# Last phase of a three-layer fp32 kernel: token tiles turned by VectorE blocks and SBUF transfers in place of TensorE transposes

## The chip, the cores and the metric

One core of one Trainium2 chip runs the whole kernel. The metric is the device time in microseconds (us); lower is better.

## What is computed

4096 tokens of width 256 pass through an attention layer, a differential cross attention and a mixture of experts, each followed by a residual sum and a layer norm. Only the last part matters here. It routes every token to two of four experts (a gated one "sw" with 1024 hidden columns, an "me" and a "ce" expert with 512, and an "ml" expert with 1024):

```python
e0 = jax.nn.silu(x @ sw_w1) * (x @ sw_w3) @ sw_w2
e1 = jax.nn.gelu(sym @ me_c1w + me_c1b, approximate=False) @ me_c2w + me_c2b
h2 = _layer_norm(syn + attn, ce_n1g, ce_n1b)
ff = jax.nn.relu(h2 @ ce_f1w + ce_f1b) @ ce_f2w + ce_f2b
h2 = _layer_norm(h2 + ff, ce_n2g, ce_n2b)
e2 = h2 @ ce_gen_w + ce_gen_b
e3 = jax.nn.gelu(x @ ml_w1 + ml_b1, approximate=False) @ ml_w2 + ml_b2
return (rw[..., None] * gathered).sum(axis=2)
```

## The kernel before, in words

Three phases run one after the other with overlaps: phase_a and phase_b are the two attention layers, phase_c is the experts. The change lies in phase_c alone. It works on `NP` = 8 "pairs" of 512 tokens. X1 holds all tokens with tokens on partitions; the matmuls need them with features on partitions, so tiles must be turned.

Every engine runs a program of its own, whose order is written out by hand. For a pair j each engine goes through `work(j, i)` for 24 chunks i of 128 hidden columns: chunks 0 to 7 are sw, 8 to 11 ce, 12 to 15 me, 16 to 23 ml. In chunk i TensorE makes `first(j, i)` (six matmuls of 512 columns, twelve for sw), ScalarE applies the activation into GF, VectorE multiplies in the gate for sw and splits the result into a high and a low fp32r half, GH (a cast at L2257 and a subtraction at L2259). TensorE then runs the second layer of chunk i-3 (`LAG` = 3), `second(24j+i-3)`: twelve matmuls of 256 columns that add up in the banks 4 and 5. Every product is made of three matmuls (`mm3`: high by high, high by low, low by high), all of which share the line L109. A first() waits for the activation that frees its bank, a second() for its GH, and the first second() of an expert also for VectorE to have taken the sums of the expert before out of the banks: `second(24j+12)` waits for `ff_add(j)` (VectorE, chunk 14), and `second(24j+16)` waits for `add_expert(j, 1)` (VectorE, chunk 18).

Three tiles a pair are turned by TensorE, each with eight 128x128 transposes into two PSUM banks; ScalarE then copies them out as the high half and VectorE subtracts to get the low half:

- `load_x(j+1)` in chunk 23 of pair j (L1881, ScalarE L2039, VectorE L2106) turns the next pair's tokens into XC, of which there is one buffer. After it TensorE runs second(24j+21) and then `synergy(j+1)`, 24 matmuls that wait for the low half.
- `turn_n(j)` in chunk 5 (L1905, L2075, L2202) turns the normalised tile NN into NTh and NTl, for chunk 8.
- `gen_turn(j)` in chunk 20 (L1914, L2080, L2202) turns the normalised residual RR, for `generate(j)` in chunk 22, 24 matmuls.

VectorE has more to do at fixed chunks: in chunk 0 the statistics of NN, in 1 its normalisation (`center`, L2158), in 2 to 4 the routing and the output norm of the pair before, in 10 and 18 an expert's sums times the routing weight (L2211), in 11 to 13 the bias rows (`add_bias`, L2219; in pair 0 in chunks 19 and 21, and instead the splits of late weights), in 14 `ff_add` (L2243), in 15 the statistics of RR and in 16 its normalisation after a wait for GpSimd's root. SyncE in this phase only stores each finished pair (after `center` in chunk 4 of the next). Pair 0 runs its first eleven chunks among the last steps of phase_b.

Of the kernel before, what the change touches and what calls it, by code (L numbers as in the profile page):

```python
# [1716 lines left out]

def in_bank(j):
    return (3, 2) if j == 0 else (7, 6)


def phase_c(M, b_end):
# [28 lines left out]
    RS = put("RSc", [128, 4])  # L1751
    XH = Place(M, 65536)("XC", [128, 2, 2, TOK], F32R)
    NN = Place(M, 81920)("NN", [128, 4, 256])
# [8 lines left out]
    d_g = {step: M.sem(f"c_g{step}") for step in LOADS}  # L1762
    d_out = M.sem("c_out")
    pe_x = M.sem("c_pe_x")
    pe_syn = M.sem("c_pe_syn")
    pe_nt = M.sem("c_pe_nt")
    pe_gt = M.sem("c_pe_gt")
    pe_gen = M.sem("c_pe_gen")
# [24 lines left out]
    dve_add = M.sem("c_dve_add")  # L1793
    dve_ff = M.sem("c_dve_ff")
    dve_seq = M.dve_seq
    pool_w = M.sem("c_pool_w")
# [9 lines left out]
    def split(w, name, q):  # L1806
# [18 lines left out]
    def sync(e):  # L1825
        w = Passed(e)

        def ask(name, q, sem):
            if name in ("sw_w1", "sw_w3", "ml_w1"):
                i = a[name].rearrange("(k p) n -> p k n", k=2)[:, :, 512 * q:512 * q + 512]  # L1830
            elif name in ("ce_f1w", "ce_gen_w"):
                i = a[name].rearrange("(k p) n -> p k n", k=2)
            else:
                i = a[name].rearrange("(k p) n -> p k n", p=128)[:, 4 * q:4 * q + 4, :]
            dma(e, RAW[name, q][:, :, :], i, sem)

        def early(s):
            if s == 238:
                for end in gathered:
                    w.wait_ge(*end)  # L1840
                for o, i in ((BC[:, 1:3, :], a["BC"][:, 1:3, :]), (bf, a["BC"][:, 3, :]), (RB[:, :, :], a["RB"]), (gc[:, :, :], a["gc"])):
                    dma(e, o, i, d_tc)
                w.wait_ge(b_end["values"], 112)
                w.wait_ge(*b_end["projected"])
            if s == 243:
                w.wait_ge(b_end["scores"], 240)
            if s == 258:
                w.wait_ge(b_end["scores"], 256)
                w.wait_ge(b_end["values"], 128)
            if s == 259:  # L1850
                w.wait_ge(b_end["folds"], 14)
            if s == 278:
                w.wait_ge(*b_end["output"])
                w.wait_ge(dve_br, 1)
            for way in LOADS.get(s, ()):
                ask(*way, d_g[s])

        def rest():
            for j in range(NP - 1):
                w.wait_ge(dve_ctr, out_stats(j) + 1)  # L1860
                dma(e, out_tm[:, 4 * j:4 * j + 4, :], X1[:, 4 * j:4 * j + 4, :], d_out)
            for u in range(2):
                t = 4 * NP - 4 + 2 * u
                w.wait_ge(dve_ctr, 3 * NP + u)
                dma(e, out_tm[:, t:t + 2, :], X1[:, t:t + 2, :], d_out)
            w.wait_ge(d_out, 16 * (NP + 1))

        return early, rest

    def tensor(e):  # L1870
# [3 lines left out]

        def load_x(j):
            w.wait_ge(b_end["normalised"], j + 1)
            for c, b in enumerate(in_bank(j)):
                if j:
                    w.wait_ge(*free[b])
                for i in range(4):  # L1880
                    t = e.transpose(P[b][:, 128 * i:128 * i + 128], X1[:, 4 * j + i, 128 * c:128 * c + 128], ident)  # L1881
                t.then_inc(pe_x, 1)
                free[b] = (dve_x, 2 * j + c + 1)

        def synergy(j):
            w.wait_ge(dve_x, 2 * j + 2)
            split(w, "ce", 0)
            wt = W["ce", 0]
            for i, b in enumerate(syn_banks(j)):
                if b > 3:  # L1890
                    w.wait_ge(*free[b])
                else:
                    w.wait_ge(act_g, 24 * (j - 1) + b + 21)
                for k in range(2):
                    t = mm3(e, P[b][:, 0:260], XH[:, k, 0, 128 * i:128 * i + 128], XH[:, k, 1, 128 * i:128 * i + 128],
                            wt[:, 0, k, :], wt[:, 1, k, :], k == 0, k == 1)
                t.then_inc(pe_syn, 1)
                free[b] = (dve_syn, 4 * j + i + 1)

        def turn_n(j):  # L1900
            w.wait_ge(dve_ctr, syn_stats(j) + 1)
            for c in range(2):
# [3 lines left out]
                t.then_inc(pe_nt, 1)  # L1906
                free[7 - c] = (dve_nt, 2 * j + c + 1)

        def gen_turn(j):
            w.wait_ge(dve_ctr, ff_stats(j) + 1)  # L1910
            for c in range(2):
                w.wait_ge(*free[7 - c])
                for i in range(4):
                    t = e.transpose(P[7 - c][:, 128 * i:128 * i + 128], RR[:, i, 128 * c:128 * c + 128], ident)  # L1914
                t.then_inc(pe_gt, 1)
                free[7 - c] = (dve_gt, 2 * j + c + 1)

# [24 lines left out]
        def first(j, i):  # L1942
            x, hc = chunk(i)
            b = first_bank(i)
            hi, lo = XH[:, :, 0, :], XH[:, :, 1, :]
            if x == "sw":
# [47 lines left out]
        def work(j, i):  # L1994
            first(j, i)
            if i == 5:
                turn_n(j)
            if i == 20:
                gen_turn(j)
            if i == 22:  # L2000
                generate(j)
            if i >= LAG:
                if i < 23 or j + 1 < NP:
                    second(24 * j + i - LAG)
            elif i and j:
                second(24 * j + i - LAG)
            if i == 23 and j + 1 < NP:
                load_x(j + 1)
                second(24 * j + 21)

        def early(s):
            if s == INPUT:
                load_x(0)
            if s == SYNERGY:
# [16 lines left out]
    def scalar(e):  # L2031
        w = Passed(e)

        def load_x(j):
            w.wait_ge(b_end["scores"], 240)
            w.wait_ge(pe_a, 24 * j)
            for c, b in enumerate(in_bank(j)):
                w.wait_ge(pe_x, 2 * j + c + 1)
                e.activation(XH[:, c, 0, :], P[b], ACT.Copy).then_inc(act_x, 1)  # L2039

# [12 lines left out]
        def work(j, i):  # L2053
# [16 lines left out]
            if i == 5:  # L2070
                w.wait_ge(b_end["folds"], 14)
                w.wait_ge(pe_gen, 4 * j)
                for c in range(2):
                    w.wait_ge(pe_nt, 2 * j + c + 1)
                    e.activation(NTh[:, c, :], P[7 - c], ACT.Copy).then_inc(act_nt, 1)  # L2075
            if i == 20:
                w.wait_ge(pe_a, 24 * j + 12)
                for c in range(2):
                    w.wait_ge(pe_gt, 2 * j + c + 1)
                    e.activation(NTh[:, c, :], P[7 - c], ACT.Copy).then_inc(act_gt, 1)  # L2080
            if i == 23 and j + 1 < NP:
                load_x(j + 1)
            if j == 0 and i in CHUNK_TAKES:
                take(*CHUNK_TAKES[i])

        def early(s):
            if s == INPUT + 1:
                load_x(0)
            if s in EARLY:
# [9 lines left out]
    def vector(e):  # L2099
        w = Passed(e)  # L2100
        seq = Chain(w, dve_seq)

        def load_x(j):
            for c, b in enumerate(in_bank(j)):
# [29 lines left out]
        def synergy(j):  # L2134
            w.wait_ge(dve_rb, 1)
            w.wait_ge(b_end["folds"], 9)
            w.wait_ge(b_end["values"], 128)
            w.wait_ge(pe_nt, 2 * j)
            for i, b in enumerate(syn_banks(j)):
# [58 lines left out]

        def turned(landed, j, done):
            for c in range(2):  # L2200
                w.wait_ge(landed, 2 * j + c + 1)
                e.tensor_tensor(NTl[:, c, :], P[7 - c], f32(NTh[:, c, :]), ALU.subtract).then_inc(done, 1)  # L2202

# [25 lines left out]
        def scaled(j):  # L2229
            w.wait_ge(dve_ctr, syn_stats(j) + 1)  # L2230
            w.wait_ge(pe_gt, 2 * j)
            w.wait_ge(*b_end["turned"])
# [13 lines left out]
        def work(j, i):  # L2246
# [18 lines left out]
            if i == 1:  # L2265
                center(syn_stats(j), NN)
            if i == 2:
                route(j)
# [4 lines left out]
            if i == 5:  # L2273
                turned(act_nt, j, dve_nt)
            if i == 20:
                turned(act_gt, j, dve_gt)
# [29 lines left out]
        def early(s):  # L2306
            if s == INPUT + 1:
                load_x(0)
            if s in DVE_TAKES:
# [258 lines left out]
```

## Time and profile before

| what | value |
|---|---|
| time, median of 3 runs | 1552.7 us (1552.16 to 1553.82) |
| span of the profiled execution | 1550.1 us |
| TensorE busy / share | 1502.6 us / 97% |
| VectorE busy / share | 1139.4 us / 74% |
| ScalarE busy / share | 847.5 us / 55% |
| mean granted TensorE clock | 0.993 |

The profiled execution is listed with its span, from the first to the last instruction; its own time is not listed apart. The median of the runs is 2.6 us above the span, which is what lies around the span. Times in the views count from the span's start. Steady pairs of phase_c repeat every 88 us from about 925 us on; the pair between 1013 us and 1101 us is looked at closely.

### The profile page before, as it was taken

How to read it: one execution, taken by the hardware profiler on the slowest of the kernel's cores; microseconds unless marked ns; L12 is line 12 of the kernel's file. 1: busy time of each engine (PE TensorE's matmuls, PEld its weight loads, DVE VectorE, ACT ScalarE, POOL GpSimd, SP SyncE). 2: the span in 40 equal slices, each digit the busy share in tenths (PEclk: the TensorE clock that was granted, in tenths of full speed). 3: DMA queues.
4: the chain of work that ended last, by engine and by line, in shares of the span. 5: the costliest groups of instructions: out<-in, count | busy, mean ns of one | idle time of the engine just before them, and what ended most of it. 6: DMA issues, size and time to landing. Idle time of an engine off the chain costs nothing.

```text
span 1550.1 us, 28824 instructions
## 1 busy us (share of the span) xinstructions
PE 1502.6 (97%) x11288; PEld 1065.1 (69%) x11288; DVE 1139.4 (74%) x2305; ACT 847.5 (55%) x1123; POOL 372.8 (24%) x404
## 2 busy tenths in 40 slices
PE   8999999899999999999999999999999999999998
PEld 4333333335566666666656898888989898888887
DVE  6445555548799999999967877777676767777675
ACT  5888889876688888888863421222222221222221
POOL 1000000124556667666453300000000000000000
PEclk9999999999899999999999999999999999999999
DMA  7656665446565666657652100000000000000000
GB/s 153 137 112 117 122 121 103 71 95 113 95 93 88 105 89 98 110 78 96 93 169 69 62 1 15 1 14 1 1 15 1 14 1 15 1 15 1 1 14 14
DMA packets 61576, 97.37 MB, mean 63 GB/s; under 512 B 12461, under 2 KB 29881, under 8 KB 61441
## 3 DMA queue, kind: packets, MB, share of 16 engines
q1 hardware_dynamic: 61312, 95.34, 33.3%
q8 instruction: 89, 1.46, 0.4%
q14 instruction: 47, 0.38, 0.1%
q10 hardware_dynamic: 128, 0.20, 0.0%
HBM read 26.29 MB, written 4.19 MB: 20 GB/s over the span
## 4 chain that ended last, share of the span: by engine, by line
PE 84%; DVE 8%; ACT 3%; SPq 3%; issue 2%; DMA 1%; POOLq 0%; DVEq 0%; POOL 0%; ACTq 0%
PE ps L109 79%; SPq L119 3%; PE ps L1277 2%; DVE NM L1495 2%; ACT H L614 1%; ACT PX L1438 1%; DVE EE L758 1%; PE ps L1239 1%; DVE XC L2106 1%; PE ps L1285 1%; PE ps L1914 0%; DMA ST<-QS 0%; PE ps L1905 0%; PE ps L1209 0%; DVE QS L678 0%
## 5 line engine op out<-in xcount | busy, mean ns | idle before, releaser
L1495 DVE TENSOR_REDUCE NM<-ps 128x4 f32<-128x1024 f32 x256 | 307.5, 1219 | 29.2 <-PE ps L109 27.7
L1438 ACT ACTIVATE PX<-ps 128x1024 f32<-128x1024 f32 x256 | 262.2, 1024 | 80.2 <-PE ps L109 79.0
L614 ACT ACTIVATE H<-ps,b1c 128x1024 f32<-128x1024 f32 x256 | 268.2, 1118 | 48.6 <-PE ps L109 47.0
L2066 ACT ACTIVATE GF<-ps,cols 128x512 f32<-128x512 f32 x128 | 88.2, 689 | 295.7 <-PE ps L109 295.6
L109 PE MATMUL ps<-XC,W_sw_w 128*128 128x512 f32 x768 | 185.8, 393 | 0.0
L2257 DVE CAST GH<-GF 128x512 fp32r<-128x512 f32 x192 | 82.0, 427 | 106.9 <-ACT GF L2066 101.8
L109 PEld LDWEIGHTS ps<-XC,W_sw_w 128*128 128x128 f32 x768 | 140.5, 188 | 28.0
L2365 POOL TENSOR_SCALAR RSc<-AGc 128x4 f32<-128x4 f32 x23 | 6.9, 298 | 599.5 <-DVE AGc L2152 599.5
L109 PE MATMUL ps<-PX,VT 128*32 128x256 f32 x2048 | 138.6, 388 | 0.1
L2259 DVE TENSOR_TENSOR GH<-GF,GH 128x512 fp32r<-128x512 f32 x192 | 133.2, 694 | 6.6
L109 PE MATMUL ps<-KT,QT 48*128 48x512 f32 x512 | 128.1, 498 | 3.7 <-DVE NM L1495 1.8
L2061 ACT ACTIVATE GF<-ps 128x512 f32<-128x512 f32 x64 | 38.0, 596 | 169.2 <-PE ps L109 169.2
L109 PE MATMUL ps<-H,w2p 128*32 128x512 f32 x1024 | 124.8, 605 | 3.0 <-ACT XF L1407 1.1
L109 PE MATMUL ps<-QT,KT 52*128 52x256 f32 x1024 | 109.2, 290 | 4.7 <-ACT PX L1438 3.8
L109 PEld LDWEIGHTS ps<-QT,KT 52*128 52x128 f32 x1024 | 90.1, 187 | 26.1 <-ACT PX L1438 10.7
L109 PE MATMUL ps<-W_ml_w,GH 128*128 128x256 f32 x768 | 103.6, 285 | 0.2
L758 DVE TENSOR_SCALAR EE<-ps,b2p 128x512 f32<-128x512 f32 x63 | 47.1, 747 | 77.0 <-PE ps L109 76.9
L109 PEld LDWEIGHTS ps<-KT,QT 48*128 48x128 f32 x512 | 47.8, 184 | 80.7 <-issue 60.2
L109 PEld LDWEIGHTS ps<-W_sw_w,GH 128*128 128x128 f32 x768 | 100.0, 191 | 4.5
L109 PE MATMUL ps<-W_sw_w,GH 128*128 128x256 f32 x768 | 102.7, 283 | 0.0
L109 PEld LDWEIGHTS ps<-W_ml_w,GH 128*128 128x128 f32 x768 | 98.0, 191 | 5.8 <-issue 3.4
L109 PE MATMUL ps<-ST,w1s 48*128 48x512 f32 x512 | 96.5, 451 | 5.3 <-ACT H L614 2.0
(240 smaller groups left out, 2560.3 us busy)
## 6 DMA issues: line engine op xcount, KB each, us to landing
KT<-KS SPq DMA_DIRECT2D x128, 192.0 KB, 4.7
ST<-QS SPq DMA_DIRECT2D x254, 96.0 KB, 2.8
QT<-XSb SPq DMA_DIRECT2D x128, 96.0 KB, 4.2
XT<-in_xT_dram SPq DMA_DIRECT2D x8, 512.0 KB, 4.1
raw_a<-in_x_dram SPq DMA_DIRECT2D x8, 512.0 KB, 4.3
CR<-in_ctxT_dram SPq DMA_DIRECT2D x8, 512.0 KB, 4.7
out_dram<-X SPq DMA_DIRECT2D x7, 512.0 KB, 2.9
R_sw_w<-in_sw_w_dram SPq DMA_DIRECT2D x6, 512.0 KB, 5.5
```

What stands on the lines that cost most here:

```text
L109: return e.matmul(o, l, r, start=start, stop=stop, skip_group_check=True)
L119: e.dma_start(o, i).then_inc(sem, 16)
L614: e.activation(H1[s % 8][:, :, :], PP[s % 3][:, :, :], ACT.Tanh, bias=b1c[:, half:half + 1], scale=1.0).then_inc(act_th, 1)
L758: e.tensor_scalar(EE[:, j % 4, :], P[6][:, :], b2p[:, 0:1], None, ALU.add).then_inc(dve_ee, 1)
L1239: t = e.transpose(low[0:32, 128 * qc:128 * qc + 128], f32(NS2[u % 2][:, 4 * qc:4 * qc + 4, :, :]).rearrange("p g l n -> p (g l n)"), ident)
L1277: t = e.transpose(P[7][:, 256 * qc + 128 * i:256 * qc + 128 * i + 128], OT[f][:, i, 128 * qc:128 * qc + 128], ident)
L1438: e.activation(PX[s % 3][:, :, :, :], PP[2][:, :, :].rearrange("p g (c q) -> p g c q", c=2), ACT.Exp, bias=0.0, scale=0.25).then_inc(act_e ...
L1495: e.tensor_reduce(NM[u % 2][:, qc, :, :, i], PP[qc][:, :, :].rearrange("p g (m k) -> p g m k", m=2), AX.X, ALU.max, negate=True).then_inc( ...
L2061: e.activation(g[:, :], o, ACT.Silu, bias=0.0, scale=1.0).then_inc(act_g, 1)
L2066: e.activation(g[:, :], o, f, bias=cols[:, col:col + 1], scale=1.0).then_inc(act_g, 1)
L2257: e.tensor_copy(h[:, 0, :], g[:, :]).then_inc(dve_h, 1)
L2259: e.tensor_tensor(h[:, 1, :], g[:, :], f32(h[:, 0, :]), ALU.subtract).then_inc(dve_h, 1)
```

## The change

Of the three turns a pair, 22 of 24 no longer use TensorE (pair 0 keeps its own load_x and turn_n). Each is now: one VectorE transpose of the 128x1024 tile in blocks of 32x32 into the new tile TT; sixteen transfers from SBUF to SBUF that put the blocks in place in the new tile XR (32 partitions, two rows of 512 bytes each, 32 KB a transfer); ScalarE's copy and VectorE's subtraction as before, but out of XR in SBUF and in runs of 32 elements.

- The turn of NN: VectorE's block in chunk 1 behind `center`, sixteen transfers by SyncE, copies in chunk 5 as before.
- The turn of the next pair's tokens: VectorE's block in chunk 8, sixteen transfers by SyncE, copies (`next_x`) in chunk 13, on VectorE ahead of add_bias. XC has two buffers. `load_x` leaves chunk 23, and second(24j+21) moves behind the next pair's synergy and its first(0).
- The turn of RR: VectorE's block in chunk 16 behind `center`, twelve transfers by SyncE and four by ScalarE (behind its activation of chunk 17, after a wait for the block), copies in chunk 20 as before.

The scratch size given to the program shrinks from its default to 1024, which makes room for TT, XR and the second XC.

```diff
+TURN_X, SPLIT_X = 8, 13
+SHARED = 3
...
+    put = Place(M, 176192)
+    XH = [Place(M, 65536)("XC0", [128, 2, 2, TOK], F32R), put("XC1", [128, 2, 2, TOK], F32R)]
+    TT = put("TT", [128, 8, 4, 32])
+    XR = put("XR", [128, 2, TOK])
...
+    def as_turned(ap):
+        return ap.rearrange("p (v a t) -> p a v t", v=4, a=4)
+    def turned(c):
+        return XR[:, c, :].rearrange("p (a v t) -> p a v t", a=4, v=4)
+    def blocks(e, rows):
+        for a in rows:
+            for b in range(4):
+                dma(e, XR[32 * b:32 * b + 32, :, 128 * a:128 * a + 128],
+                    TT[32 * a:32 * a + 32, b::4, :, :].rearrange("p c v t -> p c (v t)"), d_turn)
...
         def rest():
-            for j in range(NP - 1):
-                w.wait_ge(dve_ctr, out_stats(j) + 1)
-                dma(e, out_tm[:, 4 * j:4 * j + 4, :], X1[:, 4 * j:4 * j + 4, :], d_out)
+            for j in range(NP):
+                if j:
+                    w.wait_ge(dve_turn, n_turn(j))
+                    w.wait_ge(dve_gt, 2 * j)
+                    blocks(e, range(4))
+                    w.wait_ge(dve_ctr, out_stats(j - 1) + 1)
+                    dma(e, out_tm[:, 4 * j - 4:4 * j, :], X1[:, 4 * j - 4:4 * j, :], d_out)
+                if j + 1 < NP:
+                    w.wait_ge(dve_turn, x_turn(j + 1))
+                    w.wait_ge(dve_nt, 2 * j + 2)
+                    blocks(e, range(4))
+                w.wait_ge(dve_turn, r_turn(j))
+                w.wait_ge(dve_nt, 2 * j + 2)
+                w.wait_ge(dve_x, 2 * min(j + 2, NP))
+                blocks(e, range(SHARED))
...
             first(j, i)
-            if i == 5:
-                turn_n(j)
-            if i == 20:
-                gen_turn(j)
+            if i == 5 and not j:
+                turn_n()
                     second(24 * j + i - LAG)
-            elif i and j:
+            elif j:
                 second(24 * j + i - LAG)
-            if i == 23 and j + 1 < NP:
-                load_x(j + 1)
-                second(24 * j + 21)
...
+        def next_x(j):
+            w.wait_ge(b_end["normalised"], NP)
+            w.wait_ge(pe_a, 24 * (j - 1))
+            w.wait_ge(d_turn, 256 * x_turn(j))
+            for c in range(2):
+                e.activation(as_turned(XH[j % 2][:, c, 0, :]), turned(c), ACT.Copy).then_inc(act_x, 1)
...
                 w.wait_ge(pe_a, 24 * j + 12)
+                w.wait_ge(d_turn, 256 * r_turn(j))
                 for c in range(2):
-                    w.wait_ge(pe_gt, 2 * j + c + 1)
-                    e.activation(NTh[:, c, :], P[7 - c], ACT.Copy).then_inc(act_gt, 1)
-            if i == 23 and j + 1 < NP:
-                load_x(j + 1)
+                    e.activation(as_turned(NTh[:, c, :]), turned(c), ACT.Copy).then_inc(act_gt, 1)
+            if i == SPLIT_X and j + 1 < NP:
+                next_x(j + 1)
+            if i == 17:
+                w.wait_ge(dve_turn, r_turn(j))
+                w.wait_ge(dve_nt, 2 * j + 2)
+                w.wait_ge(dve_x, 2 * min(j + 2, NP))
+                blocks(e, range(SHARED, 4))
...
+        def next_x(j):
+            hi, lo = XH[j % 2][:, :, 0, :], XH[j % 2][:, :, 1, :]
+            for c in range(2):
                 w.wait_ge(act_x, 2 * j + c + 1)
-                e.tensor_tensor(XH[:, c, 1, :], P[b], f32(XH[:, c, 0, :]), ALU.subtract).then_inc(dve_x, 1)
+                e.tensor_tensor(as_turned(lo[:, c, :]), turned(c), f32(as_turned(hi[:, c, :])), ALU.subtract).then_inc(dve_x, 1)
+        def turn(n, tile):
+            w.wait_ge(d_turn, 256 * (n - 1))
+            e.transpose(TT[:, :, :, :].rearrange("p b v t -> p v b t"), tile.rearrange("p v (b t) -> p v b t", b=8)).then_inc(dve_turn, 1)
...
                 center(syn_stats(j), NN)
+                if j:
+                    turn_n(j)
...
-            if i == 23 and j + 1 < NP:
-                load_x(j + 1)
+            if i == TURN_X and j + 1 < NP:
+                turn_x(j + 1)
+            if i == SPLIT_X and j + 1 < NP:
+                next_x(j + 1)
...
                 center(ff_stats(j), RR)
+                turn_r(j)
...
-    nc = bacc.Bacc("TRN2", target_bir_lowering=False, num_devices=1)
+    nc = bacc.Bacc("TRN2", target_bir_lowering=False, num_devices=1, dynamic_dma_scratch_size=1024)
```

## Rows read from the trace of the kernel before

**Rows 1.** The page: busy time and share of the span of each engine, instructions.
```profile
PE 1502.6 (97%) x11288; PEld 1065.1 (69%) x11288; DVE 1139.4 (74%) x2305; ACT 847.5 (55%) x1123; POOL 372.8 (24%) x404
```
**Rows 2.** One stretch of phase_c: length, busy per engine, granted clock, DMA share, GB/s.
```profile
1000.00:1100.00 100.00, 99.80 (x641) 89.88 (x640) 68.86 (x168) 24.29 (x38) 4.42 (x6) 1.00 0.02 6
```
**Rows 3.** Chain of waits through one pair: start, length, what.
```profile
1010.89 0.45 PE ps L1881 x4
...
1038.72 0.87 PE ps L1905 x8
...
1085.27 0.87 PE ps L1914 x8
...
1098.92 0.45 PE ps L1881 x4
```
**Rows 4.** Instruction groups by line, phase_c: busy us, mean ns, idle before.
```profile
L1914 PE MATMUL ps<-C,RR 128*128 128x128 f32 x64 | 8.3, 272 | 0.0
...
L1881 PE MATMUL ps<-C,X 128*128 128x128 f32 x56 | 7.2, 272 | 0.0
L1905 PE MATMUL ps<-C,NN 128*128 128x128 f32 x56 | 7.2, 272 | 0.0
```
**Rows 5.** Timeline at a pair's end: start, length, engine, instructions, idle before.
```profile
1101.37 2.93 PEld L109 LDWEIGHTS ps<-W_ce,XC 128*128 128x128 f32 x24 [0.35 <-DVE XC L2106]
```
**Rows 6.** Instruction groups by line, VectorE, phase_c.
```profile
L2233 DVE TENSOR_TENSOR RR<-NN,BC 128x1024 f32<-128x1024 f32 x7 | 8.5, 1218 | 0.0
```
**Rows 7.** Timeline of VectorE, start of chunk 2, and chunks 8 and 9.
```profile
1026.24 0.69 DVE L2253 TENSOR_TENSOR GF<-GF,ps 128x512 f32<-128x512 f32 x1 [0.24 <-PE ps L109]
...
1052.05 0.69 DVE L2259 TENSOR_TENSOR GH<-GF,GH 128x512 fp32r<-128x512 f32 x1
1054.41 0.43 DVE L2257 CAST GH<-GF 128x512 fp32r<-128x512 f32 x1 [1.67 <-ACT GF L2066]
```
**Rows 8.** Timeline, chunks 13 to 15 (ScalarE, VectorE, TensorE), and chunk 14 of pair 0.
```profile
1065.22 0.69 ACT L2066 ACTIVATE GF<-ps,cols 128x512 f32<-128x512 f32 x1 [2.13 <-PE ps L109]
...
1066.40 0.69 DVE L2259 TENSOR_TENSOR GH<-GF,GH 128x512 fp32r<-128x512 f32 x1
1067.01 1.67 DVE L2219 SCALAR_TENSOR_TENSOR X<-BR,PB,X 128x256 f32<-128x256 f32 x4
...
1069.83 1.28 DVE L2243 TENSOR_TENSOR RR<-ps,RR 128x512 f32<-128x512 f32 x2
1071.58 0.43 DVE L2257 CAST GH<-GF 128x512 fp32r<-128x512 f32 x1 [0.47 <-ACT GF L2066]
...
1070.66 1.67 PE L109 MATMUL ps<-W_me_c2w,GH 128*128 128x256 f32 x12
...
892.70 0.43 DVE L2257 CAST GH<-GF 128x512 fp32r<-128x512 f32 x1 [0.47 <-ACT GF L2066]
```
**Rows 9.** Timeline, chunks 16 to 22 (VectorE, ScalarE, TensorE).
```profile
1076.56 1.38 DVE L2158 TENSOR_SCALAR RR<-RR,AGc,RSc 128x256 f32<-128x256 f32 x4 [0.93 <-POOL RSc L2367]
...
1079.40 0.69 ACT L2066 ACTIVATE GF<-ps,cols 128x512 f32<-128x512 f32 x1 [2.13 <-PE ps L109]
...
1081.19 1.65 DVE L2211 SCALAR_TENSOR_TENSOR X<-ps,PB,X 128x256 f32<-128x256 f32 x4
...
1082.21 1.67 PE L109 MATMUL ps<-W_ml_w,GH 128*128 128x256 f32 x12
...
1091.62 0.40 PE L109 MATMUL ps<-W_ce_gen_w,NTh 128*128 128x256 f32 x2
```
**Rows 10.** DMA issues by tile (ns min/median/max); landing of the 32 KB transfers WS (us).
```profile
L119 SPq DMA_DIRECT2D ST<-QS x254: 567/593/1848, 11.6 to 298.3; - x127
L119 ACTq DMA_DIRECT2D ST<-QS x2: 687/810/932, 13.0 to 13.8; - x2
...
L119 SPq DMA_DIRECT2D out_dram<-X x9: 372/372/392, 951.0 to 1547.5; - x9
...
DMA to landing us min/median/max: 1.9/2.7/3.7
```

More of the change, by code:

```diff
@@ L1715, in syn_banks @@
     return (2, 3, 6, 7) if j == 0 else (7, 6, 2, 3)
-def in_bank(j):
-    return (3, 2) if j == 0 else (7, 6)
+IN_BANKS = (3, 2)
+TURN_X, SPLIT_X = 8, 13
+SHARED = 3
 def phase_c(M, b_end):
@@ L1763, in phase_c @@
     d_out = M.sem("c_out")
+    d_turn = M.sem("c_turn")
     pe_x = M.sem("c_pe_x")
@@ L1766, in phase_c @@
     pe_nt = M.sem("c_pe_nt")
-    pe_gt = M.sem("c_pe_gt")
     pe_gen = M.sem("c_pe_gen")
@@ L1794, in phase_c @@
     dve_ff = M.sem("c_dve_ff")
+    dve_turn = M.sem("c_dve_turn")
     dve_seq = M.dve_seq
@@ L1813, in split, with n_turn, x_turn, r_turn @@
             w.wait_ge(pool_w, [*POOL_TAKES.values()].index((name, q)) + 1)
+    def as_turned(ap):
[7 more added lines that the diff above has]
+                    TT[32 * a:32 * a + 32, b::4, :, :].rearrange("p c v t -> p c (v t)"), d_turn)
+    def n_turn(j):
+        return max(3 * j, 0)
+    def x_turn(j):
+        return 3 * j - 2
+    def r_turn(j):
+        return 3 * j + 2 if j + 1 < NP else 3 * j + 1
     def syn_stats(j):
@@ L1873, in tensor, with load_x @@
         free[0] = free[1] = (b_end["folds"], 12)
[L1875 to L1879, printed above, removed]
+        def load_x():
+            w.wait_ge(b_end["normalised"], 1)
+            for c, b in enumerate(IN_BANKS):
                 for i in range(4):
-                    t = e.transpose(P[b][:, 128 * i:128 * i + 128], X1[:, 4 * j + i, 128 * c:128 * c + 128], ident)
+                    t = e.transpose(P[b][:, 128 * i:128 * i + 128], X1[:, i, 128 * c:128 * c + 128], ident)
                 t.then_inc(pe_x, 1)
-                free[b] = (dve_x, 2 * j + c + 1)
+                free[b] = (dve_x, c + 1)
         def synergy(j):
@@ L1906, in turn_n @@
                 t.then_inc(pe_nt, 1)
[L1907 to L1916, printed above, removed]
+                free[7 - c] = (dve_nt, c + 1)
         def generate(j):
@@ L2004, in work @@
                     second(24 * j + i - LAG)
-            elif i and j:
+            elif j:
                 second(24 * j + i - LAG)
-            if i == 23 and j + 1 < NP:
-                load_x(j + 1)
-                second(24 * j + 21)
         def early(s):
             if s == INPUT:
-                load_x(0)
+                load_x()
             if s == SYNERGY:
@@ L2032, in scalar, with load_x @@
         w = Passed(e)
-        def load_x(j):
+        def load_x():
             w.wait_ge(b_end["scores"], 240)
[L2036 to L2039, printed above, removed]
+            for c, b in enumerate(IN_BANKS):
+                w.wait_ge(pe_x, c + 1)
+                e.activation(XH[0][:, c, 0, :], P[b], ACT.Copy).then_inc(act_x, 1)
+        def next_x(j):
[4 more added lines that the diff above has]
+                e.activation(as_turned(XH[j % 2][:, c, 0, :]), turned(c), ACT.Copy).then_inc(act_x, 1)
         def take(name, q):
@@ L2072, in work @@
                 w.wait_ge(pe_gen, 4 * j)
+                if j:
+                    w.wait_ge(d_turn, 256 * n_turn(j))
                 for c in range(2):
-                    w.wait_ge(pe_nt, 2 * j + c + 1)
-                    e.activation(NTh[:, c, :], P[7 - c], ACT.Copy).then_inc(act_nt, 1)
+                    if j:
+                        e.activation(as_turned(NTh[:, c, :]), turned(c), ACT.Copy).then_inc(act_nt, 1)
+                    else:
+                        w.wait_ge(pe_nt, c + 1)
+                        e.activation(NTh[:, c, :], P[7 - c], ACT.Copy).then_inc(act_nt, 1)
             if i == 20:
                 w.wait_ge(pe_a, 24 * j + 12)
+                w.wait_ge(d_turn, 256 * r_turn(j))
                 for c in range(2):
-                    w.wait_ge(pe_gt, 2 * j + c + 1)
-                    e.activation(NTh[:, c, :], P[7 - c], ACT.Copy).then_inc(act_gt, 1)
-            if i == 23 and j + 1 < NP:
-                load_x(j + 1)
+                    e.activation(as_turned(NTh[:, c, :]), turned(c), ACT.Copy).then_inc(act_gt, 1)
[6 more added lines that the diff above has]
+                blocks(e, range(SHARED, 4))
             if j == 0 and i in CHUNK_TAKES:
@@ L2087, in early @@
             if s == INPUT + 1:
-                load_x(0)
+                load_x()
             if s in EARLY:
@@ L2101, in vector, with load_x, turn_n, turn_x @@
         seq = Chain(w, dve_seq)
-        def load_x(j):
-            for c, b in enumerate(in_bank(j)):
-                w.wait_ge(act_x, 2 * j + c + 1)
-                e.tensor_tensor(XH[:, c, 1, :], P[b], f32(XH[:, c, 0, :]), ALU.subtract).then_inc(dve_x, 1)
+        def load_x():
+            for c, b in enumerate(IN_BANKS):
+                w.wait_ge(act_x, c + 1)
+                e.tensor_tensor(XH[0][:, c, 1, :], P[b], f32(XH[0][:, c, 0, :]), ALU.subtract).then_inc(dve_x, 1)
+        def next_x(j):
+            hi, lo = XH[j % 2][:, :, 0, :], XH[j % 2][:, :, 1, :]
+            for c in range(2):
+                w.wait_ge(act_x, 2 * j + c + 1)
+                e.tensor_tensor(as_turned(lo[:, c, :]), turned(c), f32(as_turned(hi[:, c, :])), ALU.subtract).then_inc(dve_x, 1)
+        def turn(n, tile):
+            w.wait_ge(d_turn, 256 * (n - 1))
+            e.transpose(TT[:, :, :, :].rearrange("p b v t -> p v b t"), tile.rearrange("p v (b t) -> p v b t", b=8)).then_inc(dve_turn, 1)
+        def turn_n(j):
+            w.wait_ge(dve_ctr, syn_stats(j) + 1)
+            turn(n_turn(j), NN[:, :, :])
+        def turn_x(j):
+            w.wait_ge(b_end["normalised"], j + 1)
+            turn(x_turn(j), X1[:, 4 * j:4 * j + 4, :])
+        def turn_r(j):
+            w.wait_ge(dve_ctr, ff_stats(j) + 1)
+            turn(r_turn(j), RR[:, :, :])
         def take(name, q):
@@ L2137, in synergy @@
             w.wait_ge(b_end["values"], 128)
-            w.wait_ge(pe_nt, 2 * j)
+            w.wait_ge(pe_nt, 2 if j else 0)
+            w.wait_ge(dve_turn, n_turn(j - 1))
             for i, b in enumerate(syn_banks(j)):
@@ L2197, in route3, with low_n, low_r @@
             e.tensor_tensor(PB[:, :, :], LS[:, :, :], SL[:, :, :], ALU.mult).then_inc(dve_pb, 1)
-        def turned(landed, j, done):
+        def low_n(j):
             for c in range(2):
-                w.wait_ge(landed, 2 * j + c + 1)
-                e.tensor_tensor(NTl[:, c, :], P[7 - c], f32(NTh[:, c, :]), ALU.subtract).then_inc(done, 1)
+                w.wait_ge(act_nt, 2 * j + c + 1)
+                if j:
+                    e.tensor_tensor(as_turned(NTl[:, c, :]), turned(c), f32(as_turned(NTh[:, c, :])), ALU.subtract).then_inc(dve_nt, 1)
+                else:
+                    e.tensor_tensor(NTl[:, c, :], P[7 - c], f32(NTh[:, c, :]), ALU.subtract).then_inc(dve_nt, 1)
+        def low_r(j):
+            for c in range(2):
+                w.wait_ge(act_gt, 2 * j + c + 1)
+                e.tensor_tensor(as_turned(NTl[:, c, :]), turned(c), f32(as_turned(NTh[:, c, :])), ALU.subtract).then_inc(dve_gt, 1)
         def add_expert(j, k, n, count):
@@ L2230, in scaled @@
             w.wait_ge(dve_ctr, syn_stats(j) + 1)
-            w.wait_ge(pe_gt, 2 * j)
+            w.wait_ge(dve_turn, r_turn(j - 1) if j else 0)
             w.wait_ge(*b_end["turned"])
@@ L2266, in work @@
                 center(syn_stats(j), NN)
+                if j:
+                    turn_n(j)
             if i == 2:
@@ L2307, in early @@
             if s == INPUT + 1:
-                load_x(0)
+                load_x()
             if s in DVE_TAKES:
```

14 lines of the change are left out of this document (6 added, 8 removed).

## The prediction

> **What bounds the kernel now.** I read the page first: TensorE is busy for 97% of the span [rows 1]. The windows then show where the change lies: in a stretch of the last phase TensorE is busy for 99.80 of 100 us at a granted clock of 1.00 (the 2.4 GHz level), VectorE for 68.86, ScalarE for 24.29, and the DMA engines for 2% [rows 2]. So an instruction that leaves TensorE's queue there gives its time back, unless a wait takes its place. The chain of waits through one pair shows the two inner turns as eight transposes and 0.87 us each [rows 3]; the groups give their counts, 64, 56 and 56, which is eight transposes in each of 8, 7 and 7 turns [rows 4].
>
> **What is removed.** The change takes out 8 turns of RR, 7 of NN and 7 of the next tokens: 22 x 0.87 = 19.1 us. At a pair's end TensorE also stood still before synergy: the weight load waited 0.35 us for the low half of XC [rows 5]. That half is now made ten chunks earlier; 7 x 0.35 = 2.5 us. Gross gain 21.6 us. The twelve matmuls of second(24j+21) are only moved, and synergy waits for none of its banks: load_x needed the sums of generate out of the same two at the same place, and the activation of chunk 23 is over by then.
>
> **What is added on VectorE.** The trace has no VectorE transpose. Its nearest row by size is the 128x1024 tensor_tensor at 1.218 us [rows 6]; I take T = 1.22 us, with 0.85 (twice the 0.43 us of a 128x512 cast [rows 7]) and 2.4 (two passes) as ends. The copies and subtractions out of XR are taken at what they cost now, runs of 32 or not: ScalarE 0.6 us, VectorE 0.69 us alone and 0.64 us in a row, as in ff_add, two in 1.28 [rows 8]. An estimate by the Trainium skill, which has the block transposing one element per cycle and lane (Vector Engine (DVE) Microarchitecture Reference, "The reshape front-end and per-opcode configuration"), lands near T as well; no run here shows it yet.
>
> Whether this costs time depends on the chunk. In chunk 1, VectorE next waits for TensorE 0.24 us [rows 7], and TensorE gets to chunk 1 by the length of a second-layer product later than before because second(24j+21) now stands in front of it: T is covered. In chunk 8 VectorE is idle 1.67 us ahead of chunk 9 [rows 7]: covered. In chunk 13 nothing covers. The two subtractions of next_x, 1.28 us, go in ahead of add_bias, in a stretch where VectorE is full: add_bias ends at 1068.68, and ff_add starts at 1069.83, 1.15 us later, which is the cast and the subtraction of chunk 14 with no gap, its first half done near 1070.5, just when second(24j+12) starts, at 1070.66 [rows 8]. That product cannot start before ff_add has emptied its bank. With a slack of about 0.1 us **the first new wait is 1.17 us**, in six steady pairs. In pair 0 a weight split stands there instead of the bias, and VectorE is idle 0.47 us before chunk 14 [rows 8]: 0.8 us. Pair 7 has no next_x. Sum: 6 x 1.17 + 0.8 = 7.8 us.
>
> **What is added on the queues.** Transfers between SBUF tiles were issued by SyncE at 0.593 us in the median, at least 0.567; two by ScalarE took 0.687 and 0.932; the cheapest steady issue is the output's 0.372 [rows 10]. I take 0.62 us a transfer with its gap, 254 rows against two, and for ScalarE's four 2.5 us, with ends of 1.6 (0.372 and a gap, four times) and 3.3 (twice the two, with gaps). Sixteen from SyncE take 9.9 us, and the last lands some 2.7 us after its issue [rows 10].
>
> The turn of NN: center of chunk 1 ends at 1026.0 [rows 7], T at 1027.2, the last issue starts at 1036.5 and lands at 1039.2, which is where TensorE's transposes of NN end today [rows 3], three chunks before the ce expert needs them: in time. The turn of the next tokens: VectorE's chunk 8 ends at 1052.7, T to 1053.9, the last issue starts at 1063.2 and lands at 65.9; ScalarE is free from its chunk 13 at 65.91 and has both copies by 67.1; VectorE ends its chunk 13 at 67.0 [rows 8]. In time, with nothing to spare. SyncE's store of the pair before comes ahead of it, in chunk 4, and is long gone.
>
> The turn of RR is the costly one. ScalarE, after its activation of chunk 17, waits for the block and then issues four transfers; behind them in its queue stands the activation of chunk 18, behind that VectorE's chunk 18 with add_expert, and for the first two of its sums second(24j+16) waits. In the rows: center ends at 1077.94; ScalarE's chunk 18 was at 1079.40 to 1080.09; the sums began at 1081.19 and second(24j+16) at 1082.21 [rows 9]. New: 1077.94 + T 1.22 + 2.5 = 1081.66; the activation 0.69, 1082.35; then the 2.12 us that lay between the end of that activation and the product, 1084.47. **The second new wait is 2.26 us** where nothing else moved (pair 7). Where the first wait already held TensorE back by 1.17, center is late too, but only by 0.75, since VectorE's idle 0.47 us before chunk 15 swallows a part [rows 8]: 2.26 - 0.42 = 1.84 us, seven times. Sum: 7 x 1.84 + 2.26 = 15.1 us.
>
> Then generate: SyncE's twelfth issue starts near 1086.7 in pair time and lands near 1089.4; two copies and the last subtraction bring it to 1091.4. TensorE would be at generate at 1091.62 [rows 9] - 0.87 + 3.0 = 1093.8. Covered by 2.4 us, but only because of the two waits; without them it would be 0.6 us late.
>
> **The sum.** -21.6 + 7.8 + 15.1 = +1.3 us on a span of 1550.1; with the 2.6 us around the span that the median of the three runs has over it, 1554.0 us. A measurement of this kernel can tell about 0.2%, 3 us, from no change: I forecast no change that can be told.
>
> A rule speaks against the change. The row for it: a turn costs the bounding engine 0.87 us [rows 3], and VectorE's block and sixteen issues together some 11 us on other engines. The Trainium skill (VectorE: DVE Perf Modes, "Rules for kernel authors") says to turn 128x128 on TensorE if a PSUM destination is fine, and that VectorE's is only for 32x32. By the rule the gain would be nothing and the waits would stay, about 1575 us; by the row the 19.1 us come off.
>
> **Rivals.**
> (a) The forecast: both waits are there at about these prices. For it: both products start in the rows within 0.2 us of what they wait for. Its own range is 1549 to 1561: T and the four issues at their ends move eight second waits by -0.9 and +0.8 us each, -7 and +6. Chance 0.48, of which faster 0.14, same 0.19, slower 0.15.
> (b) The second wait hardly arises: ScalarE's issues run at the output's 0.37 us or are swallowed in some other way, and the wait falls under 0.5 us. Then -21.6 + 7.8 + 3 = -10.8: 1542 us. For it: 0.372 us is what SyncE pays in this very phase [rows 10]; against it: that one goes to DRAM, and ScalarE's only two rows are the dearest. Chance 0.22, faster.
> (c) Neither wait arises, because VectorE catches up more than I see: 1531 us. Against it: no gap stands between the end of add_bias and ff_add [rows 8]. Chance 0.06.
> (d) Slower: the next tokens land late. Should an issue take 0.73 us or the block 2.4, the last of sixteen lands after 1067.0, when VectorE wants it; from there each microsecond of lateness is one of TensorE's, since the copies stand ahead of the bias rows and ff_add in one queue. 0.1 us more an issue is 1.6 us later; 7 x 1.5 = 10.5 us on top: 1564 us. For it: ScalarE's rows of 0.687 and 0.932, and that SyncE's longest took 1.848 [rows 10]. Against it: the DMA engines are all but idle here [rows 2]. Chance 0.18.
> (e) The change does not shorten the pairs, because the transposes ran in the shadow of the weight loads. Against it: in the chain each eight cost 0.87 us. Then 1552.7 + 22.9 = 1576. Chance 0.06, slower, with it the rule's case.
>
> Low of the range: between (b) and (c), 1539; high: past (d), 1564. Faster by over 0.2%: 0.14 + 0.22 + 0.06 = 0.42, less what (b) loses to the middle, 0.03: 0.39. Same: 0.19 + 0.03 + 0.02 of (d) = 0.24. Slower: the rest, 0.37.
>
> **What would show it.** TensorE without the lines of the 176 transposes; in steady pairs a gap before the me expert's first second-layer product, with ff_add as its releaser, near 1.2 us, and one before the ml expert's, released by the routing sums of chunk 18, near 1.8 us; ScalarE with four issues between chunks 17 and 18 taking 2.5 us; a steady pair of 88.0 us as before [rows 3], 3.0 us saved (2 x 0.87 + 0.87 + 0.35) and 3.0 us waited. I would be wrong if ScalarE's issues take a fraction of that, if the gap is before the ce products or generate instead, or if the pair's period falls under 87 us.

## The result and the profile after

| what | before | changed |
|---|---|---|
| time, median of 4 runs | 1552.43 us (1550.18 to 1553.82) | 1560.01 us (1557.32 to 1561.39) |
| span of the profiled execution | 1550.1 us | 1559.6 us |
| TensorE busy | 1502.6 us | 1491.5 us |
| VectorE busy | 1139.4 us | 1163.0 us |

The ratio is 1.005 with a 95% interval of 1.0036 to 1.0063: 7.6 us slower, which this measurement can tell from no change. The profiled execution of the changed kernel took 1561.39 us, 1.8 us more than its span and more than the median of its runs. Where waits are added up below, they come from that execution, so its span is compared with the span before: 9.5 us more.

The page of the changed kernel, busy time of each engine, answers to [rows 1]:

```profile
PE 1491.5 (96%) x11112; PEld 1052.3 (67%) x11112; DVE 1163.0 (75%) x2327; ACT 848.4 (54%) x1123; POOL 368.9 (24%) x404
```

TensorE has 176 instructions less and is still no sooner done. One stretch of the windows, as in [rows 2] (length, busy time of TensorE, weight load, VectorE, ScalarE, GpSimd, then granted clock, DMA share, GB/s):

```profile
1000.00:1100.00 100.00, 97.33 (x602) 87.10 (x602) 73.02 (x172) 24.80 (x38) 3.79 (x6) 0.98 0.09 23
```

In 100 us TensorE now stands still for 2.67 us where it stood for 0.20, and the mean granted clock is 0.98 instead of 1.00. The waits of the last phase say for what (engine, line, for whom: us in total, times, longest):

```profile
PEld ps L109 <- DVE GH L2334: 29.5, 16, 3.1
...
PE ps L109 <- DVE X L2286: 16.6, 9, 2.7
...
PE ps L109 <- DVE RR L2318: 6.5, 7, 1.1
```

L2286 is add_expert and L2318 is ff_add; the weight loads (PEld) named in the first row are those of the same sixteen products, so their 29.5 us are not a further wait. The timeline of one steady pair shows TensorE at the two places, the me expert's first second-layer product (W_me_c2w) and the ml expert's (W_ml_w) (start, length, instructions, idle before):

```profile
1071.05 1.55 PE L109 MATMUL ps<-XC,W_me 128*128 128x512 f32 x6
1073.47 1.66 PE L109 MATMUL ps<-W_me_c2w,GH 128*128 128x256 f32 x12 [0.88 <-DVE RR L2318]
...
1083.44 1.55 PE L109 MATMUL ps<-XC,W_ml_w 128*128 128x512 f32 x6
1086.76 1.91 PE L109 MATMUL ps<-W_ml_w,GH 128*128 128x256 f32 x12 [1.77 <-DVE X L2286]
1088.46 2.76 PE L109 MATMUL ps<-XC,W_ml_w 128*128 128x512 f32 x6
```

From the start of first(15) to second(24j+12) it is 2.42 us (1073.47 less 1071.05); before it was 1.39, which is what six such matmuls take. That is 1.03 us of new wait. From first(19) to second(24j+16) it is 3.32 us (1086.76 less 1083.44) and was 1.58: 1.74 us. And the last row holds what nobody forecast: the six matmuls of first(20) take 2.76 us where the others take 1.55. The windows of that stretch give the reason (same columns as above):

```profile
1080.00:1085.00 5.00, 4.99 (x31) 4.12 (x29) 2.34 (x4) 0.76 (x2) 0.00 (x0) 1.00 0.23 57
1085.00:1086.70 1.70, 0.00 (x0) 0.00 (x0) 1.67 (x5) 0.69 (x1) 0.00 (x0) 1.00 0.18 43
1086.70:1088.40 1.70, 1.65 (x12) 1.68 (x13) 1.67 (x4) 0.00 (x0) 0.00 (x0) 0.89 0.24 58
1088.40:1091.00 2.60, 2.60 (x8) 2.04 (x7) 0.05 (x1) 0.00 (x0) 0.00 (x0) 0.50 0.10 25
```

TensorE was busy at 2.4 GHz, stood still for 1.7 us, began again, and then was granted 0.50, the 1.2 GHz level, although it was at work. That the standstill brought the lower clock is only a reading of these rows; the experiments below test it.

The chain of waits through the second wait of this pair names every link (start, length, what):

```profile
1078.36 1.39 DVE RR L2225 x4
1079.74 0.02 issue
1079.77 1.26 DVE TT L2160
1081.02 0.02 issue
1081.04 0.60 ACTq L119
1081.64 0.03 issue
1081.67 0.87 ACTq L119
1082.54 0.03 issue
1082.57 0.62 ACTq L119
1083.19 0.03 issue
1083.22 0.63 ACTq L119
...
1083.95 0.70 ACT GF L2099
```

Center, the block, ScalarE's four issues, and only then the activation of chunk 18, as the forecast had them. The instructions and issues of the new tile (ns min/median/max, first and last start, shape) give their prices:

```profile
L119 SPq DMA_DIRECT2D XR<-TT x320: 585/597/1573, 878.1 to 1532.5; - x160
L119 ACTq DMA_DIRECT2D XR<-TT x32: 596/625/872, 905.2 to 1527.7; - x32
L2160 DVE STREAM_TRANSPOSE TT<-RR x8: 1245/1245/1247, 904.0 to 1524.2; 128x1024 f32<-128x1024 f32 x8
...
DMA to landing us min/median/max: 1.8/1.9/3.8
```

Last, pair 0. Its timeline of TensorE shows a wait before the ce expert's first second-layer product, which started at 883.26 us without one before:

```profile
884.62 1.68 PE L109 MATMUL ps<-W_ce_f2w,GH 128*128 128x256 f32 x12 [1.15 <-DVE X L2286]
...
897.26 1.67 PE L109 MATMUL ps<-W_me_c2w,GH 128*128 128x256 f32 x12 [1.12 <-DVE RR L2318]
...
910.95 1.67 PE L109 MATMUL ps<-W_ml_w,GH 128*128 128x256 f32 x12 [2.17 <-DVE X L2286]
```

Its wait before the me product has a cause of its own besides VectorE's queue. Timeline of ScalarE: the two copies of next_x wait for GpSimd, which has just normalised the last tokens, and VectorE's subtractions wait for the copies.

```profile
892.09 1.15 ACT L2072 ACTIVATE XC<-XR 128x512 fp32r<-128x512 f32 x2 [0.86 <-POOL X L1664]
```

### The profile page after: what moved, and what is told of

It reads as the page before. It is cut to its first block, busy times and chain, and to the rows that moved or that the text cites. A ratio compares the mean times of both kernels' runs of the same rounds, so it can differ in the third digit from the quotient of the medians.

```text
span 1559.6 us, 28882 instructions
## 1 busy us (share of the span) xinstructions
PE 1491.5 (96%) x11112; PEld 1052.3 (67%) x11112; DVE 1163.0 (75%) x2327; ACT 848.4 (54%) x1123; POOL 368.9 (24%) x404
## 3 DMA queue, kind: packets, MB, share of 16 engines
q10 hardware_dynamic: 2688, 1.25, 0.4%
## 4 chain that ended last, share of the span: by engine, by line
PE 75%; DVE 12%; ACT 4%; issue 3%; SPq 2%; ACTq 1%; DMA 1%; POOL 1%; POOLq 0%; DVEq 0%
PE ps L109 72%; SPq L119 2%; PE ps L1277 2%; DVE NM L1495 2%; ACTq L119 1%; ACT H L614 1%; ACT PX L1438 1%; DVE GH L2332 1%; ACT GF L2099 1%; DVE TT L2160 1%; DVE EE L758 1%; DVE GH L2334 1%; DVE RR L2225 1%; DVE X L2294 1%; PE ps L1239 1%
## 5 line engine op out<-in xcount | busy, mean ns | idle before, releaser
L1438 ACT ACTIVATE PX<-ps 128x1024 f32<-128x1024 f32 x256 | 262.2, 1024 | 80.0 <-PE ps L109 79.0
L109 PEld LDWEIGHTS ps<-W_ml_w,GH 128*128 128x128 f32 x768 | 101.3, 194 | 22.7 <-DVE GH L2334 18.6
L109 PE MATMUL ps<-XC,W_ml_w 128*128 128x512 f32 x384 | 104.1, 409 | 0.0
```

Source lines behind the costliest of these rows:

```text
L109: return e.matmul(o, l, r, start=start, stop=stop, skip_group_check=True)
L1438: e.activation(PX[s % 3][:, :, :, :], PP[2][:, :, :].rearrange("p g (c q) -> p g c q", c=2), ACT.Exp, bias=0.0, scale=0.25).then_inc(act_e ...
```

## The experiments

The theory after the result: the loss is the two waits, plus the lower clock that follows the longer of them. Rivals: the blocks load VectorE too much by themselves; the transfers are late; ScalarE's issues overlap other work; the lower clock has a cause of its own. All edits are against the changed kernel except where it is said. Times are medians. The first four experiments were measured on one chip and the other three on another, each time together with the kernel before (1552.22 us on the first chip, 1550.84 on the second), and each ratio is to the kernel before on the same chip. A "standstill" is the idle time of TensorE before one of its products.

### ScalarE issues one chunk later

```diff
-            if i == 17:
+            if i == 18:
                 w.wait_ge(dve_turn, r_turn(j))
```

> ScalarE issues its four transfers behind its activation of chunk 18 instead of chunk 17. Theory of the two waits: nothing that second(24j+16) needs stands behind the issues any more, so the 1.9 us it waits (2.2 in pair 0) fall under 0.2 us in all eight pairs, 8 x 1.8 = 14 us, and the stretches at the lower clock that follow this wait in some pairs (1.5 us each) go with it: about 1541 us, and a steady pair of 86.1 us. Wait before second(24j+12) stays at 1.0 us. Rival, that the block's 1.25 us on VectorE is what delays chunk 18: the wait stays above 1 us and the time above 1550. Rival, that the lower clock comes from something other than TensorE's standing still: the slow stretches stay, about 1546.

Measured: 1538.59 us, ratio to the kernel before 0.9914 (0.9899 to 0.9928). TensorE at the same two products of a steady pair, timeline, weight loads:

```profile
1065.20 1.49 PEld L109 LDWEIGHTS ps<-W_me_c2w,GH 128*128 128x128 f32 x12 [1.27 <-DVE GH L2334]
...
1076.74 1.49 PEld L109 LDWEIGHTS ps<-W_ml_w,GH 128*128 128x128 f32 x12 [0.43 <-issue]
```

The first wait is as long as in the changed kernel (1.27 us in the weight load there too), the second has shrunk from 2.17 to 0.43 us, and 990.62 to 1076.74 us is a pair of 86.12 us. No stretch of the last phase shows a lower clock. So it was the place of ScalarE's issues, not the block and not the transfers, that made the second wait, and the lower clock went with the standstill. The size fits too: the ratios to the kernel before, 0.9914 and 1.005, are some 21 us apart, and the second waits (15.3 us) and four falls of the clock (6.2 us, both added up below) are 21.5.

### All transfers by SyncE

```diff
-SHARED = 3
+SHARED = 4
```

> All sixteen transfers of the residual go out on SyncE, none on ScalarE (SHARED 4). Theory of the two waits: the wait before second(24j+16) falls under 0.2 us, but the last of sixteen issues at 0.64 us starts 9.6 us behind the block and lands 1.9 us later; two copies and the last subtraction make the low half ready some 1.3 us after TensorE gets to generate. The wait moves there: 8 x (1.8 - 1.3) = 4 us and the slow stretches less, 1552 us, about the time of the kernel before. Rival, that the transfers have room: no wait before generate and 1541 us.

Measured: 1552.98 us, ratio 0.9996 (0.9982 to 1.0011). Timeline of TensorE, its only idle times in a pair:

```profile
1072.44 1.67 PE L109 MATMUL ps<-W_me_c2w,GH 128*128 128x256 f32 x12 [0.88 <-DVE RR L2318]
1084.14 1.67 PE L109 MATMUL ps<-W_ml_w,GH 128*128 128x256 f32 x12 [0.18 <-DVE X L2286]
1094.69 0.50 PE L109 MATMUL ps<-W_ce_gen_w,NTh 128*128 128x256 f32 x2 [1.85 <-DVE NTl L2277]
```

The wait moved, as expected, from the ml product to generate. This pair has the longest; over the eight pairs it is 0.54 to 1.85 us, 10.0 us together and 1.25 in the mean, against 1.3 expected. So some of the sixteen transfers are needed on a second queue; only their place was wrong.

### Bias rows late in all pairs

```diff
-    return 16 if j else 4
+    return 4
...
-            w.wait_ge(dve_add, ADDS * j + 4 * k + (0 if j else 4))
+            w.wait_ge(dve_add, ADDS * j + 4 * k + 4)
...
-            for k in (BIASES if j else FIRST_BIASES).get(i, ()):
+            for k in FIRST_BIASES.get(i, ()):
```

> All pairs add their bias rows as pair 0 does, in chunks 19 and 21 instead of 11 to 13, so that next_x meets a VectorE with room. Theory of the two waits: the wait of 1.0 us before second(24j+12) goes in the pairs 1 to 6, and stays in pair 0; the wait before second(24j+16) grows by 0.3 to 0.4, to 2.3 us, since center no longer hides behind it: net 6 x 0.65 = 4 us, 1556 us, or less of it if the longer standstill brings the lower clock in more pairs (then 1560). Rival, that ff_add is late for another reason than VectorE's queue, such as the transfers landing late: the wait stays.

Measured: 1566.22 us, ratio 1.0088 (1.0073 to 1.0104): slower than the changed kernel, though one of its waits is gone. Timeline of TensorE:

```profile
1076.16 1.50 PEld L109 LDWEIGHTS ps<-W_me_c2w,GH 128*128 128x128 f32 x12 [0.24 <-issue]
...
1090.49 2.90 PE L109 MATMUL ps<-W_ml_w,GH 128*128 128x256 f32 x12 [2.79 <-DVE X L2286]
```

The first wait is gone in the pairs 1 to 6, so VectorE's full queue in chunk 13 made it there. But the second grew by 1.0 us, to 2.79, not by 0.3 to 0.4: it took over the whole of the first. Removing 1.03 us at one place brought 1.0 back at the next, and with the longer standstill the lower clock came in 6 pairs instead of 4 (the twelve matmuls at 1.67 us took 2.90). My expectation was short by both.

### Both edits together

> Both edits together: issues behind chunk 18 and bias rows late. Theory of the two waits: neither wait is left in the steady pairs, a steady pair takes 88.0 - 3.0 = 85.0 us, only pair 0 keeps its waits before the ce and the me expert (2.4 us together): 1552.4 - 21.6 + 2.4 = 1533 us. Rival, that a third wait stands just behind these two (generate, or the sums of chunk 18 behind the block): above 1540.

Measured: 1539.82 us, ratio 0.9904 (0.9876 to 0.9933); three runs near 1540 and one of 1531.78. Its last phase was as expected: no wait at either product after pair 0, and most pairs of 85.1 to 85.2 us. Some at least of the missing 7 us lay elsewhere. Windows before the last phase, the profiled execution of this run:

```profile
350.00:375.00 25.00, 25.00 (x101) 12.76 (x102) 14.56 (x17) 6.64 (x11) 6.57 (x7) 0.53 0.50 69
```

A granted clock of 0.53 for 25 us, in a phase none of the edits touches. The same kernel was measured again, on the second chip:

> The kernel with both edits once more. In its profiled run a stretch of 25 us near 360 us, in a phase that no edit touches, ran at a granted clock of 0.53 where the kernel before had 1.00. If that stretch comes and goes, most runs stand near 1532 us, as one of four did; if it belongs to this kernel, most stand near 1540 again. The steady pair stays at 85.2 us either way.

Measured: 1534.66 us, ratio 0.9892 (0.9859 to 0.9924), all six runs between 1530.29 and 1536.53. The same window:

```profile
350.00:375.00 25.00, 23.78 (x172) 13.01 (x171) 22.34 (x26) 12.93 (x19) 11.84 (x12) 1.00 0.71 102
```

The slow stretch does not belong to the kernel, since the same kernel ran without it. Whether the chip or chance sets it off was not tried. The kernel before has such a spread as well: on the second chip its runs lie between 1545.13 us, at a mean granted clock of 0.998, and 1559.52, at 0.986.

The two traces of this kernel show one more thing of that sort, on TensorE near 865 us, where the last phase overlaps with the one before:

```profile
867.44 0.41 PE L1285 MATMUL ps<-C,ON 128*128 128x128 f32 x2 [2.48 <-DVE NTl L2272]
867.60 4.59 PE L109 MATMUL ps<-XC,W_sw_w 128*128 128x512 f32 x12
```

```profile
864.05 0.41 PE L1285 MATMUL ps<-C,ON 128*128 128x128 f32 x2 [2.47 <-DVE NTl L2272]
864.21 3.02 PE L109 MATMUL ps<-XC,W_sw_w 128*128 128x512 f32 x12
```

The first two rows are from the first trace, the others from the second. After the same standstill the same twelve matmuls took 1.57 us longer in one of them. All nine traces, the kernel before included, have this standstill of 2.47 to 2.48 us; the long matmuls follow it in two, here and in the kernel with late bias rows.

This version beats both kernels: 1.1% below the kernel before and, by the two ratios, some 1.6% below the changed one. Its time can't be told from that of the kernel with ScalarE's issues one chunk later (0.9914); its pairs are shorter, 85.2 against 86.1 us.

### Eight issues on ScalarE

```diff
-SHARED = 3
+SHARED = 2
```

> ScalarE issues eight transfers in chunk 17 instead of four (SHARED 2), the rest as in the changed kernel. Theory that ScalarE's issues stand ahead of chunk 18 one for one: four more at 0.73 us are 2.9 us more before second(24j+16) in each pair, 4.7 us in a steady pair and 5.6 us in pair 7; 8 x 2.9 = 23 us, and the lower clock follows in every pair instead of every second, 4 x 1.5 = 6 us: 1589 us. Rival, that ScalarE's issues overlap its wait for the block: under 1575.

Measured: 1592.88 us (2 runs), ratio 1.027 (1.0216 to 1.0325). Timeline of ScalarE and of TensorE in one pair:

```profile
1090.68 5.41 ACTq L119 DMA_DIRECT2D XR<-TT  x8
1096.19 1.27 ACT L2099 ACTIVATE GF<-ps,cols 128x512 f32<-128x512 f32 x2 [6.48 <-issue]
...
1099.00 2.75 PE L109 MATMUL ps<-W_ml_w,GH 128*128 128x256 f32 x12 [4.38 <-DVE X L2286]
```

Four more issues lengthen the standstill from 1.77 to 4.38 us, 2.6 us or 0.65 us an issue (0.73 was expected), and the lower clock follows in all eight pairs. The issues stand ahead of chunk 18 one for one.

### VectorE's blocks alone

Against the kernel before: the block transposes at their three places into a spare tile that nobody reads.

```diff
+        def block(tile):
+            seq.wait()
+            seq.done(e.transpose(TT[:, :, :, :].rearrange("p b v t -> p v b t"), tile.rearrange("p v (b t) -> p v b t", b=8)))
...
                 center(ff_stats(j), RR)
+                w.wait_ge(dve_ctr, ff_stats(j) + 1)
+                block(RR[:, :, :])
```

> The kernel before with VectorE's block transposes added at their three places, writing a spare tile that nobody reads; TensorE still turns everything and there are no transfers. Theory: the block's 1.25 us are hidden in the chunks 1, 8 and 16 of steady pairs, whose period stays at 88.0 us to within 0.3; pair 0, whose VectorE also splits weights, loses 1.1 us before the ce expert's first second-layer product: 1552.4 + 1.1 = 1553.5 us. Rival, that the blocks themselves delay the sums of chunk 18: 0.5 us or more a pair, over 1556.

Measured: 1552.66 us, ratio 1.0012 (0.9989 to 1.0034). Timeline of TensorE, the one new wait and two pairs' ends:

```profile
882.99 1.67 PE L109 MATMUL ps<-W_ce_f2w,GH 128*128 128x256 f32 x12 [1.16 <-DVE X L2212]
...
1013.16 2.94 PEld L109 LDWEIGHTS ps<-W_ce,XC 128*128 128x128 f32 x24 [0.35 <-DVE XC L2107]
1101.29 2.94 PEld L109 LDWEIGHTS ps<-W_ce,XC 128*128 128x128 f32 x24 [0.35 <-DVE XC L2107]
```

A steady pair takes 88.13 us with 3.7 us more work on VectorE, against 88.0 without: the blocks are hidden. In pair 0 the block of chunk 8 is not, and costs the 1.16 us seen in the changed kernel.

### Standstill and clock over all runs

| TensorE's standstill before second(24j+16), or before generate where it says so | pairs followed by the 1.2 GHz level |
|---|---|
| under 0.5 us (issues behind chunk 18) | 0 of 8 |
| 0.5 to 1.9 us, before generate (all transfers by SyncE) | 0 of 8 |
| 1.7 to 1.8 us (changed kernel, pairs 1 to 6) | 3 of 6 |
| 2.2 us (pair 0 of the changed kernel and of the one with late bias rows) | 0 of 2 |
| 2.7 to 2.8 us (pair 7 of the changed kernel, pairs 1 to 7 with late bias rows) | 7 of 8 |
| 4.3 to 5.4 us (eight issues) | 8 of 8 |

Each such fall costs about 1.56 us in the changed kernel: in its chain of waits (start, length, what) the stretch behind the product is 63.72 us long where the clock fell and 62.16 us where it did not:

```profile
998.90 62.16 PE ps L109 x384
...
1086.76 63.72 PE ps L109 x384
```

Pair 7 of the changed kernel agrees: its first twelve matmuls after the wait took 2.46 us instead of 1.67, the next six 2.34 instead of 1.57, 1.56 us more together.

In the changed kernel the three standstills of 1.77 to 1.79 us were followed by the fall and the three of 1.73 were not. Length alone does not decide it, though: 1.85 us before generate and 2.17 in pair 0 had no fall behind them, and the 2.48 us near 865 us had one in two traces of nine. What decides is open. That the falls need a long standstill is shown: without the second wait there were none in the last phase, and with 4.3 us and more there was one every time.

## Why the prediction was right, and where it was not

The time lay in the range and the mechanism was the forecast one: the gross gain is eaten up by the two waits of rival (a). The point forecast, no change that can be told, was missed by 6 us: 1554.0 forecast, 1560.0 measured, and by the forecast's own measure of 3 us that is a change. That the range held is in part luck. Its upper end of 1564 was made for late tokens (rival (d)), which cost about 0.3 us, and not for the clock, which took up that room. In the profiled execution:

- **The gross gain**, 21.6 us, was nearly right. The kernel with both edits, which keeps the whole removal and hardly a wait, has pairs of 85.2 us, 2.8 us under the 88.0 of [rows 3]; the forecast was 3.0. Rival (e) and the rule of the Trainium skill (VectorE: DVE Perf Modes, "Rules for kernel authors") to turn 128x128 tiles on TensorE both fell with it: where TensorE is the bound, turning by VectorE and transfers took 1.1% off the kernel once the waits were gone. In the changed kernel itself it did not pay.
- **VectorE's block** was taken at 1.22 us and took 1.245. Its cover in chunks 1 and 8 of steady pairs held. The blocks alone show that, and that in chunk 16 too it costs nothing as long as no issue of ScalarE waits for it.
- **The first wait** was 1.17 us a pair and 7.8 in all; measured 1.03 in five steady pairs, 1.28 in pair 0 and about 1.3 in pair 5: 7.7 us. Pair 0 was forecast at 0.8; its copies waited for GpSimd, which the forecast had left out. In pair 5 one of SyncE's issues took 1.28 us and the tokens landed late, in the way of rival (d) (chain of waits: start, length, what):

```profile
1329.52 1.28 SPq L119
```

- **The second wait** was 1.84 us a pair and 15.1 in all; measured 6 x 1.74, 2.14 in pair 0 and 2.7 in pair 7: 15.3 us. Two of its terms were off and nearly cancelled in steady pairs, which is luck; in pair 7, where only the first of them acts, it was 2.7 against 2.26. ScalarE's four issues took 2.9 us, not 2.5, from 1081.04 to 1083.95. And center was not late by 0.75 us: first(15) started 1.78 us later than before and center 1.80 (1078.36 against 1076.56 in [rows 9]), so it was late by 0.02. I had let VectorE's 0.47 us idle before chunk 15 swallow a part of the delay and had left out the 0.93 us that center used to wait for GpSimd, which stands in the same rows. The experiment with late bias rows shows what follows from that: the first wait costs nothing by itself as long as the second stands behind it.
- **The step that failed** is the sum, which had no term for TensorE's clock. The forecast read 1.00 in [rows 2] and carried it over to a kernel with standstills. Four falls of 1.56 us are 6.2 us, the greater part of the 8.2 us between the forecast +1.3 and the measured +9.5 in the spans.
- **A term left out**: the block of chunk 8 was called covered by the 1.67 us idle of a steady pair. Pair 0 has weight splits there, and it cost 1.1 us.
- **Slips of the working**: with the four issues at their ends, -7 and +6 us around 1554.0 are 1547 to 1560, not 1549 to 1561, and the ends of T are not in them. The remark that generate would be 0.6 us late without the two waits did not come true: the kernel with both edits waited there once, 0.28 us in one trace and 0.15 in the other. The forecast had the transfers land 2.7 us after their issue, and they landed after 1.9. And 2.6 us were put around the span where an execution has 1.8.

Together: -21.6 + 7.7 + 15.3 + 1.1 + 6.2 = +8.7 us, of 9.5 between the two spans; 0.2 us lie before the last phase. The 0.6 left are not shown at one place. By an estimate the somewhat smaller gross gain covers them: the pair of 87.95 us is 0.15 above 88.03 - 3.0 + 1.03 + 1.74, and there are seven pairs after the first.

Rival (b), that ScalarE's issues come nearly free, was wrong: 0.63 us each, one for one. Rival (c), no wait at all, was wrong. What the forecast said to look for was all there: the two gaps with their releasers, the four issues between the activations of chunks 17 and 18, and a pair of 87.9 us (998.90 less 910.95 us is 87.95) where the clock held.

## What to carry to other kernels

Before work is taken off the bounding engine, follow each queue that takes it over to the next instruction for which that engine waits: here four issues of 0.6 us on ScalarE, put one chunk too early, cost 15 us and what followed, and one chunk later they cost nothing. Two waits in one chain need not be a sum: here taking the first away only fed the second, so cure the last first. And price a standstill of TensorE above its length where it comes near 2 us: here the clock fell behind half of those of 1.7 to 1.8 us and nearly all of those above 2.7, at 1.56 us each.

## What was not expected of the hardware

- TensorE's granted clock fell to the 1.2 GHz level after standstills of only 1.7 to 1.8 us in half of the cases, some 1.7 us after it had begun again, though it had been busy without a gap for over 11 us before the standstill. Standstills of up to 1.4 us never did it in the last phase of the traces, and some of 1.9 and 2.2 us did not either. One of 2.48 us at the same place of every trace did it in two of nine.
- A transfer of 32 KB between SBUF tiles landed 1.9 us after its issue and cost its queue 0.60 us on SyncE and 0.63 on ScalarE; the second of each four on ScalarE took 0.87.
- The block transpose of 128x1024 fp32 elements on VectorE took 1.245 us, about what a tensor_tensor of that size takes (1.218 in [rows 6]), with both sides read and written in runs of 32.
